# Attention block's drain: batches 3 to 5 placed before the last residual, second choices placed in a step of their own

## The chip, the cores and the metric

The kernel runs on one core of a Trainium2 chip. The metric is the device time of one execution in microseconds; the number given for a kernel is the median of its runs. A core has five engines that run side by side and meet only at semaphores: TensorE (PE, matrix products and transposes), VectorE (DVE), ScalarE (ACT), GpSimd (POOL, which here issues the indirect DMAs that gather and scatter rows) and SyncE (SP, which issues the plain DMAs).

## The reference

Eight batches of 512 rows with 128 columns (4096 rows in all) go through three layers, each added to its input: half an expert layer, linear attention, half an expert layer again.

```python
x = x + 0.5 * ffn(layernorm(x))          # experts
x = x + attn(layernorm(x))               # linear attention, 16 heads of 8
x = x + 0.5 * ffn(layernorm(x))          # experts again

def ffn(x):
    logits = xt @ wg                                     # [4096, 8]
    topv, topi = top_k(softmax(logits), 2)               # two experts for each row
    flat = one_hot(topi.T, 8).reshape(2 * 4096, 8)       # all first choices, then all second ones
    pos = sum((cumsum(flat, axis=0) - 1) * flat)         # place of the row in its expert's buffer
    valid = pos < 1024                                   # capacity; what is over is dropped
    disp[topi, pos] = xt ; y = relu(disp @ w1 + b1) @ w2 + b2
    return sum(gate * y[topi, pos])
```

What matters here is the order in the running sum: the place of a first choice depends on the first choices of the rows before it only; the place of a second choice depends on all first choices and on the second ones before it.

## The kernel before

The program has four blocks one after the other: the first routing, the first expert layer, attention with the second routing, and the second expert layer. `f` in the code is 0 for the first expert layer and 1 for the second. A batch g is four tiles of 128 rows, tiles 4g to 4g+3; all of x stays on chip in `x_sb`.

The attention block is a software pipeline over the batches, written out by hand as one list for each engine; an engine does its list strictly in order. For a batch: DVE adds the gathered expert rows to x (`add_rows`), gives statistics; ACT normalises; PE transposes and projects to q, k, v (`q`, `kv`), makes the key sums (`keysum`) and the answers (`query`); DVE divides (`divide`, L1425); PE turns and projects the result (`turn_out`, `project`, L1205 and L1209); DVE adds it to x (`residual`, L1431) and takes row statistics (`statistics`, L1437). After the loop over the batches comes the drain: what is left of batches 6 and 7, and of the routing.

The second routing runs in the same block behind it (class `Route`). For each batch PE turns x (`turn`, L467) and makes logits (`row_logits`, L479), ACT copies both (`turned_out` L426, `raw_out` L431). Then, for a part of the batches (`PARTS[1]`: part 0 is batches 0 to 2, part 1 batches 3 to 5, part 2 batches 6 and 7), DVE makes

- the mean and inverse deviation of each row from the statistics (`row_scalar_steps`, L253 to L295, small dependent steps on 8 or 12 columns),
- the two choices (`top2_steps`, L557 to L590; L575 gives the first choice and the semaphore `first_chosen`),
- the places (`place_steps`, L692 to L722) out of counts that PE makes with a triangular matrix and one of ones (`early_counts` L667 and L668, `late_counts` L674 and L675); L702 is the scan that reads them, L722 gives `place` and the semaphore `rows_placed`,
- the gap of the two logits (`gap_steps`, L728 and L733), of which ACT takes the exponential (`scalar_gate`, L451), and then gate and target number of each row, written beside the row (`first_marks`, L741 to L750).

These are Python generators: the list of DVE weaves the steps of two or three of them together, since each waits for its own step before. ACT writes the normalised rows (`scalar_norm`, L416).

POOL runs `dispatch`. For a part it waits for `rows_placed`, for both marks and, batch by batch, for the rows (`norm_act`); then it issues one indirect DMA for each tile, which scatters 128 rows to `xs_dram` at their places (L770, 32 for the first choices). Then the marks are rewritten for the second choice (`second_marks`, L759 and L760, which wait until the first scatters of that part have landed), and 32 more scatters go out (L775).

The second expert layer starts with a read of `xs_dram` (SP, `sync_rows`, L839), which waits for all 64 scatters. Before it PE does 36 transposes that serve nothing but to keep it busy (`WARM`, L948); they wait for the 28th scatter of a second choice. Then come sixteen steps of 512 rows (L904 to L940), the scatter of the results (L880) and the sums (L863).

Before the change part 2 places the first choices of batches 6 and 7 and all second choices in one step (40 columns of tiles), since `last_part` in `place_steps` stands for part 2.

Of the kernel before, what the change touches and what calls it, by code (L numbers as in the profile page):

```python
# [30 lines left out]
P = 128  # L31
NB, SEQ, C = 8, 512, 128
N = NB * SEQ
NT = N // P
GT = SEQ // P
NG = NT // GT
E, K, H = 8, 2, 512
# [4 lines left out]
PARTS = ((0, NG // 2, NG), (0, NG - 5, NG - 2, NG))  # L42
# [36 lines left out]
def finish(steps):  # L79

    for _ in steps:
        pass


def advance(steps, n):

    for _ in range(n):
        next(steps, None)


def macaron(nc, x_in, Wq, bq, Wk, bk, Wv, bv, Wo, bo, wg, w1, b1, w2, b2, out):
    ctx = ExitStack()
    with ctx:
        def sb(name, shape, dt=F32):
            return ctx.enter_context(nc.sbuf_tensor(name, shape, dt))
# [35 lines left out]
        token_id = sb("token_id", [P, NT])  # L131
        token_row = sb("token_row", [P, K, NT])
        carry = sb("carry", [P, E, K * NT])
        carry_early = [sb(f"carry_early{p}", [P, E, GT * PARTS[1][p + 1]]) for p in range(2)]
        head_mask = sb("head_mask", [P, HEADS])
        block_mask = sb("block_mask", [P, P])
        zeros = sb("zeros", [P, GT, C])
# [220 lines left out]
        class Route:  # L358
# [302 lines left out]
            def early_counts(self, pe, part):  # L661

                n = GT * PARTS[1][part + 1]
                pe.wait_ge(first_chosen, part + 1)
                pe.wait_ge(qT_ready, NG - 1 + part)
                by_expert = self.choice[:, 0:n].rearrange("p j e -> p e j")
                nc.tensor.matmul(bank[1][:, 0:E * n].rearrange("p (e j) -> p e j", e=E), tri[:], by_expert, start=True, stop=True)  # L667
                nc.tensor.matmul(bank[1][:, 256:256 + E * n].rearrange("p (e j) -> p e j", e=E), ones_bf[:], by_expert, start=True, stop=True).then_inc(counts_done, 1)  # L668
# [8 lines left out]
            def place_steps(self, dve, ch, part):  # L677
# [1 line left out]

                last_part = part == len(PARTS[1]) - 2
                n = K * NT if last_part else GT * PARTS[1][part + 1]
                js = slice(GT * PARTS[1][part], n)
                w = js.stop - js.start
# [76 lines left out]
            def dispatch(self, gp):  # L762

                for part in range(3):
                    gp.wait_ge(rows_placed, part + 1)
                    gp.wait_ge(first_marked, 2 * part + 2)
                    for g in range(PARTS[1][part], PARTS[1][part + 1]):
                        gp.wait_ge(norm_act, NG + g + 1)
                        for t in range(GT * g, GT * g + GT):
                            gp.indirect_dma_start(out=xs_dram, out_offset=bass.IndirectOffsetOnAxis(ap=self.place[:, t:t + 1], axis=0),  # L770
                                                  in_=self.xns[:, g, t % GT], in_offset=None).then_inc(firsts_in[part], 16)
                for part in range(3):
                    gp.wait_ge(second_marked, 2 * part + 2)
                    for t in range(GT * PARTS[1][part], GT * PARTS[1][part + 1]):
                        gp.indirect_dma_start(out=xs_dram, out_offset=bass.IndirectOffsetOnAxis(ap=self.place[:, NT + t:NT + t + 1], axis=0),  # L775
                                              in_=self.xns[:, t // GT, t % GT], in_offset=None).then_inc(seconds_in[t // (NT - GT)], 16)
# [344 lines left out]
        class Attention:  # L1121
# [21 lines left out]
            def tensor(self, pe):  # L1143
# [56 lines left out]
                def project(n):  # L1200
                    if n >= 1:
                        pe.wait_ge(x_summed, n)
                    if n >= 2:
                        pe.wait_ge(raw_ready, min(n - 1, NG - 3))
                    nc.tensor.matmul(bank[7].rearrange("p (t c) -> p t c", c=C), ones2[:], bpair[:].unsqueeze(1).to_broadcast([2, GT, C]), start=True, stop=False)  # L1205
                    pe.wait_ge(attT_ready, n + 1)
                    for t in range(GT):
                        at = slice(t * P, (t + 1) * P)
                        last = nc.tensor.matmul(bank[7][:, at], self.attT[:, n % 2, at], WT[:, 3], start=False, stop=(t == GT - 1))  # L1209
                    last.then_inc(o_ready, 1)  # L1210
# [30 lines left out]
                project(NG - 2)  # L1241
                turn_out(NG - 1)
                project(NG - 1)
                self.route.turn(pe, NG - 2)
                self.route.row_logits(pe, NG - 2)
                self.route.turn(pe, NG - 1)
                self.route.row_logits(pe, NG - 1)
                self.route.early_counts(pe, 1)
                self.route.late_counts(pe)

            def scalar(self, act):
# [37 lines left out]
                def attT_out(n):  # L1289
                    act.wait_ge(att_turned, n + 1)  # L1290
                    if n >= 2:
                        act.wait_ge(o_ready, n - 1)
                    nc.scalar.copy(self.attT[:, n % 2], bank[6][:]).then_inc(attT_ready, 1)
# [26 lines left out]

                self.route.raw_out(act, NG - 3)
                attT_out(NG - 1)
                self.route.turned_out(act, NG - 2)
                self.route.raw_out(act, NG - 2)
                self.route.turned_out(act, NG - 1)
                self.route.raw_out(act, NG - 1)
                self.route.scalar_norm(act, 3)
                self.route.scalar_norm(act, 4)
                self.route.scalar_gate(act, 1)
                self.route.scalar_norm(act, 5)  # L1330
                self.route.scalar_gate(act, 2)
                self.route.scalar_norm(act, 6)
# [2 lines left out]
            def vector(self, dve, ch):  # L1335
# [146 lines left out]
                den_max(NG - 2)  # L1482
                den_inverse(NG - 2)
                divide(NG - 2)
                k_sum(NG - 1)
                q_sum(NG - 1)
                kv_mask(NG - 1)
                advance(scalars, 8)
                den_max(NG - 1)
                den_inverse(NG - 1)  # L1490
                divide(NG - 1)
                residual(NG - 2)
                statistics(NG - 2)
                advance(scalars, 3)
                residual(NG - 1)
                statistics(NG - 1)
                ranks = route.top2_steps(dve, ch, 1)
                for _ in scalars:
                    advance(ranks, 1)
                scalars = row_scalar_steps(ch, dve, GT * PARTS[1][2], NT)  # L1500
                for _ in ranks:
                    advance(scalars, 2)
                finish(route.gap_steps(dve, ch, 1))
                placing = route.place_steps(dve, ch, 1)
                for _ in placing:
                    advance(scalars, 1)
                finish(scalars)
                ranks = route.top2_steps(dve, ch, 2)
                for _ in route.first_marks(dve, ch, 1):
                    advance(ranks, 1)  # L1510
                finish(ranks)
                placing = route.place_steps(dve, ch, 2)
                for _ in route.gap_steps(dve, ch, 2):
                    advance(placing, 1)
                advance(placing, 2)
                for _ in route.first_marks(dve, ch, 2):
                    advance(placing, 1)
                finish(placing)
                for part in range(3):
                    route.second_marks(dve, part)  # L1520

# [200 lines left out]
```

## Time and profile before

| | |
|---|---|
| median of 3 runs | 512.05 us (510.95 to 512.68) |
| the profiled execution | 511.76 us |
| its span in the trace | 509.9 us, 1.86 us less than its time |
| PE busy | 331.7 us, 65% |
| DVE busy | 339.5 us, 67% |
| ACT busy | 236.2 us, 46% |
| POOL busy | 270.9 us, 53% |
| 64 scatters of rows (L770, L775) | 62.1 us of POOL |
| 64 scatters of results (L880) | 70.3 us of POOL |

The span is what the trace covers; the device time is a little more. No engine is busy for the whole span, so the busy shares don't say what sets the end. In the map of the span in 40 slices (12.75 us each) PE is at nought tenths in slices 25 to 28, about 306 to 357 us: there only POOL works. The scatters of the second routing lie at 279 to 369 us. What a change there is worth is read from that stretch alone.

### The profile page before, as it was taken

The numbers are of one execution on the slowest core, as the hardware profiler recorded it, in microseconds if no ns is written. First come the engines' busy times: TensorE is split into PE (matmuls) and PEld (weight loads), VectorE is DVE, ScalarE is ACT, GpSimd is POOL, SyncE is SP. The second block draws the span as 40 slices with busy tenths as digits, with TensorE's granted clock in tenths as the row PEclk, the third lists the DMA queues.
The fourth block names the chain that finished last, engine by engine and source line by source line (L and its number), as shares of the span: only waits on it lengthen the run. The fifth ranks groups of instructions, "written<-read, shape, count | busy, mean of one in ns | idle before, by whom it ended". The sixth has DMA issues, their size and how long they took to land. (4 is left out here: it accounts for less than half of the span.)

```text
span 509.9 us, 5878 instructions
## 1 busy us (share of the span) xinstructions
PE 331.7 (65%) x1679; PEld 266.7 (52%) x1679; DVE 339.5 (67%) x1035; ACT 236.2 (46%) x430; POOL 270.9 (53%) x302
## 2 busy tenths in 40 slices
PE   7913489999999205678779830000479999999600
PEld 6902178888888103556657710000458888888400
DVE  6788579888787325689989782000057888888673
ACT  3687056666666103456548451000046666666200
POOL 9000777655630077667650737777603666666730
PEclk9999999999999755799988955555589999999955
DMA  8920114665554412112110101111131222221399
GB/s 238 356 90 0 37 50 145 194 187 183 188 189 158 163 51 53 47 46 53 42 42 1 54 22 52 52 54 52 51 127 36 84 81 82 84 63 41 117 335 282
DMA packets 43632, 53.32 MB, mean 105 GB/s; under 512 B 6646, under 2 KB 27152, under 8 KB 43600
## 3 DMA queue, kind: packets, MB, share of 16 engines
q1 hardware_dynamic: 30720, 33.69, 20.2%
q0 software_dynamic: 8512, 17.15, 11.6%
q10 hardware_dynamic: 4368, 2.10, 1.4%
q8 instruction: 14, 0.23, 0.2%
q14 instruction: 18, 0.15, 0.1%
HBM read 25.52 MB, written 27.39 MB: 104 GB/s over the span
## 5 line engine op out<-in xcount | busy, mean ns | idle before, releaser
L981 ACT ACTIVATE hf<-psum,bcol 128x512 f32<-128x512 f32 x128 | 88.5, 692 | 65.5 <-PE psum L918 62.4
L890 POOL DMA_INDIRECT xg<-xn_dram,gidx x64 | 65.1, 1017 | 68.1 <-POOLq L1541 38.0
L880 POOL DMA_INDIRECT yt_dram<-y_sb,target x64 | 70.3, 1099 | 51.8 <-DVE y_sb L1031 36.5
L1018 DVE TENSOR_TENSOR hl<-hf,hh 128x512 fp32r<-128x512 f32 x128 | 87.0, 692 | 4.5 <-ACT hh L983 2.0
L1118 POOL DMA_INDIRECT yg<-y_dram,slot x64 | 60.7, 949 | 25.1 <-issue 18.7
L916 PE MATMUL psum<-xh,wres 128*128 128x512 f32 x128 | 54.9, 429 | 2.8 <-DVE xl L1007 2.8
L1007 DVE TENSOR_TENSOR xl<-psum,xh 128x512 fp32r<-128x512 f32 x32 | 21.9, 684 | 51.9 <-ACT xh L966 51.9
L966 ACT CAST xh<-psum 128x512 fp32r<-128x512 f32 x32 | 18.8, 588 | 75.9 <-PE psum L904 73.7
L929 PE MATMUL psum<-hh,wres 128*128 128x512 f32 x128 | 52.8, 413 | 0.0
L918 PE MATMUL psum<-xh,wres 128*128 128x512 f32 x128 | 51.6, 403 | 0.0
L917 PE MATMUL psum<-xl,wres 128*128 128x512 f32 x128 | 51.6, 403 | 0.0
L930 PE MATMUL psum<-hl,wres 128*128 128x512 f32 x128 | 50.3, 393 | 0.0
L931 PE MATMUL psum<-hh,wres 128*128 128x512 f32 x128 | 50.3, 393 | 0.0
L1011 DVE CAST hh<-hf 128x512 fp32r<-128x512 f32 x96 | 41.7, 435 | 12.0 <-ACT hf L981 10.1
L770 POOL DMA_INDIRECT xs_dram<-xns,place x32 | 31.1, 971 | 32.5 <-DVE xns L750 15.8
L948 PE MATMUL psum<-ident 128*128 128x128 f32 x36 | 5.6, 333 | 58.7 <-DMA xs_dram<-xns,place 58.7
L948 PEld LDWEIGHTS psum<-ident 128*128 128x128 f32 x36 | 5.4, 178 | 60.5 <-DMA xs_dram<-xns,place 60.5
L775 POOL DMA_INDIRECT xs_dram<-xns,place x32 | 31.0, 969 | 9.8 <-issue 9.4
L1343 DVE SCALAR_TENSOR_TENSOR x_sb<-yg,gate,x_sb 128x128 f32<-128x128 f32 x64 | 18.1, 344 | 21.5 <-DMA yg<-y_dram,slot 21.4
L1257 ACT ACTIVATE an<-x_sb,rsa 128x128 f32<-128x128 f32 x32 | 13.2, 484 | 36.4 <-DVE rsa L1387 36.4
L916 PEld LDWEIGHTS psum<-xh,wres 128*128 128x128 f32 x128 | 25.1, 196 | 7.9 <-DVE xl L1007 3.4
L918 PEld LDWEIGHTS psum<-xh,wres 128*128 128x128 f32 x128 | 24.9, 194 | 6.1
(221 smaller groups left out, 734.6 us busy)
## 6 DMA issues: line engine op xcount, KB each, us to landing
yt_dram<-zeros SPq DMA_DIRECT2D x24, 256.0 KB, 3.4
ring<-yt_dram SPq DMA_DIRECT2D x24, 256.0 KB, 5.0
xs_dram<-blank SPq DMA_DIRECT2D x16, 260.0 KB, 3.1
xg<-xs_dram SPq DMA_DIRECT2D x16, 260.0 KB, 2.7
wexp_raw<-in_L_ffn_w SPq DMA_DIRECT2D x16, 256.0 KB, 6.0
y_dram<-y_sb SPq DMA_DIRECT2D x16, 256.0 KB, 2.4
x_sb<-in_L_attn_x SPq DMA_DIRECT2D x8, 256.0 KB, 4.0
xn_dram<-xns SPq DMA_DIRECT2D x8, 256.0 KB, 6.2
```

The lines of the kernel that those rows point to most:

```text
L880: gp.indirect_dma_start(out=yt_dram, out_offset=bass.IndirectOffsetOnAxis(ap=target[:, j:j + 1], axis=0), in_=self.y_sb[:, s % YG, t], in_ ...
L890: gp.indirect_dma_start(out=self.xg[:, s % 4, t], out_offset=None, in_=xn_dram, in_offset=bass.IndirectOffsetOnAxis(ap=gidx[:, j:j + 1], a ...
L916: nc.tensor.matmul(bank[1 + c][:], w[:, 0, at], self.xh[:, s % 2], start=True, stop=False)
L917: nc.tensor.matmul(bank[1 + c][:], w[:, 0, at], self.xl[:, s % 2], start=False, stop=False)
L918: nc.tensor.matmul(bank[1 + c][:], w[:, 2, at], self.xh[:, s % 2], start=False, stop=True).then_inc(h_ready[c], 1)
L929: nc.tensor.matmul(sums[:], w[:, 1, at], self.hh[:, s % 2, c], start=(c == 0), stop=False)
L930: nc.tensor.matmul(sums[:], w[:, 1, at], self.hl[:, s % 2, c], start=False, stop=False)
L931: last = nc.tensor.matmul(sums[:], w[:, 3, at], self.hh[:, s % 2, c], start=False, stop=(c == HC - 1))
L981: one = nc.scalar.activation(self.hf[:, c], bank[1 + c][:], ACT.Relu, bias=bcol[:, at:at + 1])
L1011: dve.tensor_copy(self.hh[:, s % 2, c], self.hf[:, c]).then_inc(hh_ready[c], 1)
L1018: dve.tensor_tensor(self.hl[:, s % 2, c], self.hf[:, c], self.hh[:, s % 2, c].bitcast(F32), ALU.subtract).then_inc(hl_ready[c], 1)
L1118: gp.indirect_dma_start(out=self.yg[:, n % YB, k, t], out_offset=None, in_=y_dram, in_offset=bass.IndirectOffsetOnAxis(ap=slot[:, k, GT * ...
```

## The change

Five things are changed:

- The second choices become a fourth step of placing: `last_part` is now part 3 with 32 columns, and part 2 places the 8 tiles of batches 6 and 7 alone, with a third mask `carry_early` (128 partitions x 256 elements, set once at the start of the kernel).
- PE makes counts for part 1 right after the projection of batch 7, before batch 6 is turned for the routing, and a third pair of early counts for part 2.
- ACT normalises batches 3 and 4 and takes the exponential for part 1 before it copies the turned rows of batches 6 and 7.
- DVE starts on the row scalars of part 1 sooner, chooses and places part 1 between the division of batch 7 and the last residual, and does part 2 and the second choices after that.
- POOL waits for the fourth `rows_placed` before the first scatter of a second choice.

```diff
-                pe.wait_ge(qT_ready, NG - 1 + part)
+                pe.wait_ge(qT_ready, NG - 1 if part == 0 else NG)
+                if part > 0:
+                    pe.wait_ge(counts_read, part)
...
-                last_part = part == len(PARTS[1]) - 2
+                last_part = part == len(PARTS[1]) - 1
...
+                gp.wait_ge(rows_placed, 4)
                 for part in range(3):
                     gp.wait_ge(second_marked, 2 * part + 2)
...
                 project(NG - 1)
+                self.route.early_counts(pe, 1)
                 self.route.turn(pe, NG - 2)
...
-                self.route.early_counts(pe, 1)
+                self.route.early_counts(pe, 2)
                 self.route.late_counts(pe)
...
                 attT_out(NG - 1)
+                self.route.scalar_norm(act, 3)
+                self.route.scalar_gate(act, 1)
+                self.route.scalar_norm(act, 4)
                 self.route.turned_out(act, NG - 2)
...
                 divide(NG - 2)
+                advance(scalars, 6)
                 k_sum(NG - 1)
                 q_sum(NG - 1)
                 kv_mask(NG - 1)
-                advance(scalars, 8)
+                advance(scalars, 6)
                 den_max(NG - 1)
                 den_inverse(NG - 1)
                 divide(NG - 1)
+                ranks = route.top2_steps(dve, ch, 1)
+                advance(ranks, 3)
                 residual(NG - 2)
-                statistics(NG - 2)
-                advance(scalars, 3)
-                residual(NG - 1)
-                statistics(NG - 1)
...
+                placing = route.place_steps(dve, ch, 1)
+                for _ in route.gap_steps(dve, ch, 1):
+                    advance(placing, 1)
+                advance(placing, 3)
+                for _ in route.first_marks(dve, ch, 1):
+                    advance(placing, 1)
+                finish(placing)
+                residual(NG - 1)
+                statistics(NG - 2)
+                statistics(NG - 1)
...
+                finish(route.place_steps(dve, ch, 3))
                 for part in range(3):
                     route.second_marks(dve, part)
```

On DVE before the change, from the division of batch 7 (L1425) on: both residuals (L1431) with their statistics come first, then the choices of part 1 (L557 to L575).

```order
L1425 TENSOR_TENSOR att<-psum,den 128x512
L1431 TENSOR_TENSOR x_sb<-psum,x_sb 128x512
L1437 BN_STATS stats<-x_sb 128x6 x4
L291 SCALAR_TENSOR_TENSOR nw<-nw 128x12
...
L1431 TENSOR_TENSOR x_sb<-psum,x_sb 128x512
L1437 BN_STATS stats<-x_sb 128x6 x4
L291 SCALAR_TENSOR_TENSOR nw<-nw 128x12
L557 TENSOR_REDUCE first<-raw 128x12
```

After the change, the same engine from the same division on (L1429 and L1435 are the same lines, four further down; `first` and `top` are maxima of the choosing, `place` the result of placing part 1):

```order
L1429 TENSOR_TENSOR att<-psum,den 128x512
L557 TENSOR_REDUCE first<-raw 128x12
L561 TENSOR_TENSOR ranked<-raw,first 128x96
L565 TENSOR_TENSOR ranked<-ranked,prefer 128x96
L1435 TENSOR_TENSOR x_sb<-psum,x_sb 128x512
L569 TENSOR_REDUCE top<-ranked 128x12
...
L752 TENSOR_SCALAR xns<-gap 128x12
L724 TENSOR_TENSOR place<-valid,slotf 128x12
L1435 TENSOR_TENSOR x_sb<-psum,x_sb 128x512
L1441 BN_STATS stats<-x_sb 128x6 x8
```

One residual and eight statistics now stand behind the placing of part 1 instead of ahead of its first step; the other residual stands inside the choosing.

On PE before, from the projection of batch 7 on (L1209): two batches turned and their logits, then the counts of part 1 (192 columns) and the late counts (512).

```order
L1209 MATMUL psum<-WT,attT 128x128 x4
L467 MATMUL psum<-ident,x_sb 128x128 x4
L479 MATMUL psum<-wgc,xT 128x8 x4
L467 MATMUL psum<-ident,x_sb 128x128 x4
L479 MATMUL psum<-wgc,xT 128x8 x4
L667 MATMUL psum<-choice,tri 128x192
L668 MATMUL psum<-choice,ones_bf 128x192
L674 MATMUL psum<-choice,tri 128x512
L675 MATMUL psum<-choice,ones_bf 128x512
```

After, from the same projection on (L1212); L669 and L670 are the early counts:

```order
L1212 MATMUL psum<-WT,attT 128x128 x4
L669 MATMUL psum<-choice,tri 128x192
L670 MATMUL psum<-choice,ones_bf 128x192
L467 MATMUL psum<-ident,x_sb 128x128 x4
L479 MATMUL psum<-wgc,xT 128x8 x4
L467 MATMUL psum<-ident,x_sb 128x128 x4
L479 MATMUL psum<-wgc,xT 128x8 x4
L669 MATMUL psum<-choice,tri 128x256
L670 MATMUL psum<-choice,ones_bf 128x256
L676 MATMUL psum<-choice,tri 128x512
L677 MATMUL psum<-choice,ones_bf 128x512
```

The counts of part 1 moved ahead of four groups of matrix products, and a pair with 256 columns is new.

## Rows read from the trace of the kernel before

**Rows 1.** Chain that ended last, 366 to 373 us: start, us, what.

```profile
366.84 2.34 DMA xs_dram<-xns,place
369.28 2.74 DMA xg<-xs_dram
372.06 0.67 PE psum L904 x4
```

**Rows 2.** Timeline of POOL: start, us, instruction, [idle before it <- releaser].

```profile
279.31 1.01 POOL L770 DMA_INDIRECT xs_dram<-xns,place  x1 [15.82 <-DVE xns L750]
...
293.38 0.97 POOL L770 DMA_INDIRECT xs_dram<-xns,place  x1 [0.30 <-issue]
301.88 0.97 POOL L770 DMA_INDIRECT xs_dram<-xns,place  x1 [7.53 <-ACT xns L416]
...
326.09 0.97 POOL L770 DMA_INDIRECT xs_dram<-xns,place  x1 [0.30 <-issue]
...
366.84 0.97 POOL L775 DMA_INDIRECT xs_dram<-xns,place  x1 [0.30 <-issue]
```

**Rows 3.** Timeline of DVE, 278 to 301 us.

```profile
278.32 0.18 DVE L750 TENSOR_SCALAR xns<-gap 128x12 f32<-128x12 f32 x1
...
285.41 0.17 DVE L253 TENSOR_TENSOR nw<-stats 128x12 f32<-128x12 f32 x1
...
287.53 0.22 DVE L1414 TENSOR_SCALAR den<-psum 128x64 f32<-128x64 f32 x1
...
288.37 0.69 DVE L1425 TENSOR_TENSOR att<-psum,den 128x512 f32<-128x512 f32 x1
289.13 0.69 DVE L1431 TENSOR_TENSOR x_sb<-psum,x_sb 128x512 f32<-128x512 f32 x1
...
291.64 0.69 DVE L1431 TENSOR_TENSOR x_sb<-psum,x_sb 128x512 f32<-128x512 f32 x1 [0.41 <-PE psum L1209]
...
293.23 0.25 DVE L557 TENSOR_REDUCE first<-raw 128x12 f32<-128x96 f32 x1
...
293.51 0.26 DVE L561 TENSOR_TENSOR ranked<-raw,first 128x96 f32<-128x96 f32 x1
...
297.82 0.25 DVE L693 TENSOR_TENSOR pos<-choice,expert_base 128x96 f32<-128x96 bf16 x1
...
298.46 0.56 DVE L702 TENSOR_TENSOR_SCAN cum<-psum,carry_early 128x191 f32<-128x191 f32 x1
...
300.33 0.17 DVE L722 TENSOR_TENSOR place<-valid,slotf 128x12 int32<-128x12 f32 x1
...
300.96 0.17 DVE L750 TENSOR_SCALAR xns<-gap 128x12 f32<-128x12 f32 x1
```

**Rows 4.** Timeline of PE, 285 to 297 us.

```profile
285.54 1.25 PE L1189 MATMUL psum<-kv,qT 128*128 128x144 f32 x8 [0.46 <-DVE kv L1410]
...
287.93 1.16 PE L1209 MATMUL psum<-WT,attT 128*128 128x128 f32 x8
...
290.45 1.16 PE L1209 MATMUL psum<-WT,attT 128*128 128x128 f32 x8
291.44 0.60 PE L467 MATMUL psum<-ident,x_sb 128*128 128x128 f32 x4
...
296.17 0.50 PE L667 MATMUL psum<-choice,tri 128*128 128x192 bf16 x1
296.49 0.52 PE L668 MATMUL psum<-choice,ones_bf 128*128 128x192 bf16 x1
```

**Rows 5.** Timeline of ACT, normalised rows of batches 3 and 4.

```profile
296.44 3.19 ACT L416 ACTIVATE xns<-x_sb,nmr,rstd 128x128 f32<-128x128 f32 x8
```

**Rows 6.** Stretches: length, busy PE, PEld, DVE, ACT, POOL, clock, DMA, GB/s.

```profile
196.00:213.50 17.50, 12.13 (x36) 8.49 (x37) 10.38 (x49) 5.77 (x11) 12.60 (x14) 0.60 0.19 51
374.00:377.40 3.40, 3.28 (x10) 2.69 (x11) 0.98 (x4) 1.27 (x2) 0.00 (x0) 0.50 0.34 129
```

**Rows 7.** Timeline of POOL in the expert layer, 470 us.

```profile
470.58 1.36 POOL L880 DMA_INDIRECT yt_dram<-y_sb,target  x1 [0.30 <-issue]
```

More of the change, by code:

```diff
@@ L133, in macaron @@
         carry = sb("carry", [P, E, K * NT])
-        carry_early = [sb(f"carry_early{p}", [P, E, GT * PARTS[1][p + 1]]) for p in range(2)]
+        carry_early = [sb(f"carry_early{p}", [P, E, GT * PARTS[1][p + 1]]) for p in range(3)]
         head_mask = sb("head_mask", [P, HEADS])
@@ L1326, in scalar @@
                 self.route.raw_out(act, NG - 1)
-                self.route.scalar_norm(act, 3)
-                self.route.scalar_norm(act, 4)
-                self.route.scalar_gate(act, 1)
                 self.route.scalar_norm(act, 5)
@@ L1491, in vector @@
                 divide(NG - 1)
+                ranks = route.top2_steps(dve, ch, 1)
+                advance(ranks, 3)
                 residual(NG - 2)
-                statistics(NG - 2)
-                advance(scalars, 3)
-                residual(NG - 1)
-                statistics(NG - 1)
[L1497 to L1500, printed above, removed]
                 for _ in ranks:
[L1502 to L1505, printed above, removed]
                     advance(scalars, 1)
                 finish(scalars)
+                placing = route.place_steps(dve, ch, 1)
[8 more added lines that the diff above has]
+                statistics(NG - 1)
+                scalars = row_scalar_steps(ch, dve, GT * PARTS[1][2], NT)
                 ranks = route.top2_steps(dve, ch, 2)
-                for _ in route.first_marks(dve, ch, 1):
-                    advance(ranks, 1)
-                finish(ranks)
+                advance(scalars, 4)
+                for _ in ranks:
+                    advance(scalars, 1)
+                finish(scalars)
                 placing = route.place_steps(dve, ch, 2)
@@ L1514, in vector @@
                     advance(placing, 1)
-                advance(placing, 2)
+                advance(placing, 3)
                 for _ in route.first_marks(dve, ch, 2):
```

## The prediction

> **What bounds the kernel now.** I read the chain of waits first, then the timeline of POOL through the second routing, and then what DVE, PE and ACT do while POOL stands still. The chain ends the attention block with POOL's last scatter of rows, its landing, one read by SP and the first transposes of the expert layer [rows 1]. Nothing else stands in that chain for a long way back: the issues of the 64 scatters follow each other. From the issue at 326.09 to the last one at 366.84 there are 32 steps [rows 2], so one costs 40.75/32 = 1.273 us. Only two breaks are in the row of 64: the start, and 7.53 us ahead of 301.88. Part 0 (12 scatters, 279.31 to 293.38) is done by 294.35, and part 1 is not ready. From 301.88 on POOL never stops: 51 steps of 1.274 us make 64.96, which is 366.84. So each microsecond by which the issue at 301.88 comes sooner moves the last one by a microsecond, as long as every later part is ready in time. At most 7.53 - 0.30 = 7.23 us can be had, since 0.30 us lies between any two issues.
>
> What does POOL wait for at 301.88? The row names ACT's normalised rows. But the first four scatters of part 1 need batch 3 only, and batches 3 and 4 were written from 296.44 to 299.63 [rows 5], so ACT had long been done for them. What came last is DVE: place at 300.33 + 0.17 = 300.50 and the marks at 300.96 + 0.17 = 301.13 [rows 3]. From the marks to the issue is 0.75 us; for part 0 it is 279.31 - 278.50 = 0.81 [rows 2, 3]. I take 0.78 from "ready" to "issued".
>
> **Where DVE loses its time before, and when part 1 is ready after.** All times are those of the profiled execution.
>
> Step 1, the division. PE's answers for batch 7 end at 285.54 + 1.25 = 286.79 [rows 4], but DVE reads them at 287.53 [rows 3], because eight steps of row scalars stand ahead, from 285.41 on, 2.12 us. Six steps now go before the keys of batch 7, into idle time of DVE, and only six are left here; the dependent ones take 0.2 us each, 1.2 in all. DVE reads at about 286.85, 0.68 us sooner; the division, at 288.37 before, starts at 287.69. Its next instruction can start 0.64 us later, 288.33.
>
> Step 2, three steps of choosing. One dependent step on 96 elements takes 293.51 - 293.23 = 0.28 us [rows 3], with small steps woven in or not; I take 0.29. The third starts at 288.9, and the residual of batch 6 at 289.15. PE's projection for it ends at 287.93 + 1.16 = 289.09 [rows 4], so it isn't waited for, and the residual is where it was (289.13). It holds DVE 0.6 us, to 289.75. Thus PE's projection of batch 7, which needs that residual, stays at 290.45 to 291.61.
>
> Step 3, the rest of the choosing: seven steps of 0.29 and 0.16 to the next free instruction make 2.19, to 291.94; the first instruction of placing starts at 292.03. Before it was at 297.82. The 5.8 us between are the two statistics and the last residual, which waited 0.41 us for PE [rows 3], the row scalars of part 2, and the 0.68 of step 1: all of that now stands behind.
>
> Step 4, placing and marks: before it is 2.68 us from 297.82 to the end of place and 3.31 to the end of the marks, which came last. Now marks and placing are woven, so place ends last: 292.03 + 2.65 = 294.68. With 0.78 the issue comes at 295.46 instead of 301.88: **6.42 us sooner**. POOL would still be idle for 1.1 us.
>
> What must be there by then: (a) The scan L702 comes 0.6 us after placing starts, 292.6; PE's counts follow the projection of batch 7, can start at 291.44 like the transposes there before, and took 0.84 us from 296.17 to 297.01 [rows 4]: 292.3, a margin of 0.3 us, the smallest. It delays the turning of batch 6 by as much, which isn't on the path. (b) ACT's rows of batch 3: the row scalars end at 291, four activations take half of 3.19 us [rows 5], 292.6, then the exponential 0.2; DVE asks for it at 293.8. Margin 1 us. (c) Part 2 must be ready 12 issues after 295.46, that is by 310.7 - 0.8 = 309.9. DVE: last residual and eight statistics to 297.1. ACT copies the turned rows of batch 6 only at 294.4 (behind batch 4) and the residual of batch 7 comes 3 us later than before; turning and logits of 7 then take 2.9 us, so raw logits at 298.9. Ten steps of choosing 3.0, placing of 8 tiles about 2.8: 304.7. Margin 5 us, so the longer way costs nothing. (d) The second choices need 32 columns placed after that, below 5.6 us, 310.3, and are asked for at 295.46 + 20 x 1.273 - 0.8 = 320.1. The new wait on POOL thus costs nothing; nothing but those 32 scatters is queued behind it. (e) New work: a third mask at the start of the kernel and a pair of matmuls, beside work that isn't waited for; between 0 and 0.5 us, the longer of the marks of the mask being POOL's alone; I take 0.
>
> What POOL gives back then passes on: the last landing, SP's read and PE's start depend on nothing that stays in place, and the expert layer behind is one rigid piece. Span 509.9 - 6.42 = 503.5, and with the 1.86 outside the trace 505.3. The profiled execution (511.76) is 0.29 under the median of the runs (512.05), so for the median **505.6 us**.
>
> **A rule to weigh.** In these rows each of the twelve scatters of part 0 took 0.97 to 1.01 us while DVE was at work nearly all the time, and in the expert layer one took 1.36 [rows 2, 7]. The Trainium skill (SBUF — State Buffer, Who interferes with whom) says that a copy, cast or tensor_scalar of VectorE can hold the port through which GpSimd writes descriptors, and then the issue waits. By that rule POOL's issues at 295 to 310 us, which move beside a DVE that is placing, would be longer. The small steps of the routing didn't do that before, so the trace speaks against it here; the fourth rival below prices it.
>
> **Rivals.**
> 1. More is gained. If the reckoned 294.68 is a microsecond too late, POOL's pause closes: 7.23 us, 504.8. Beside it the clock: at the start of the expert layer PE ran at the lower level, 1.2 GHz (0.50), for the 3.4 us from 374.0 with PE busy for 3.28 [rows 6]. Had it not fallen after the 36 transposes, half of that, 1.7 us, is won too: 503.1. The transposes move with the scatters, so I see no reason for either sign, and hold it as spread.
> 2. Less is gained. The margin (a) of 0.3 us fails, or the chain on DVE is longer than its steps, or the clock rises 3.3 us later in the expert layer (1.65 us lost). For it: four engines hand over to each other within 8 us. One to three us: 506.8 to 508.6.
> 3. Nothing or a loss: the clock. The restart of PE in the attention block had a mean of 0.60 over 17.5 us with PE busy for 12.1 [rows 6]. If the expert layer, now begun at another moment, stood at 1.2 GHz for long, every microsecond there would cost half a one. The point is 13 us beyond the 3.4: then the 6.42 are gone; at 20 us the time is 505.6 + 10 = 515.6. Against it: PE was busy without a break from 374.12 on, and rose at 377.4.
> 4. The port. 11 issues between 295.5 and 309.9, each longer by 1.36 - 0.97 = 0.39, cost 4.3 us: 509.9.
> 5. The change does not do what it says, because part 2 is late. It would have to come at 309.9 + 6.4 = 316.3 to take all, 11.6 us after what I reckon.
>
> **How the numbers follow.** Forecast 505.6 with its own range 504.4 to 506.8 (0.6 for the steps, as much for the clock and the spread of the runs): 0.70. Rival 1: 0.12. Rival 2: 0.11. Rival 4: 0.02. Rivals 3 and 5: 0.05, of which 0.03 end slower and 0.02 within 0.3%. A measurement of this kernel can tell 0.3% (1.5 us) from no change. For 8 in 10 the range reaches into rivals 1 and 2: 503.7 to 508.2. Faster by over 0.3% (under 510.5) are the forecast, 1, 2 and 4: 0.95; same 0.02; slower 0.03.
>
> **What would show it.** POOL's thirteenth scatter of rows starts near 295.5 with an idle of 1.1 us before it, and 51 steps of 1.27 us follow without a break to about 360.4. On DVE the first line of choosing starts near 288.3, placing near 292.0, place ends near 294.7. PE's counts of part 1 end by 292.3. The first transposes of the expert layer are at 365.6 instead of 372.06. Step 1 is wrong if the division doesn't move; step 3 if DVE waits for raw logits or for the residual's projection; (a) if the scan has idle time with PE as its releaser; (c) or (d) if POOL pauses a second time. The whole is wrong if the expert layer takes longer than before from its first transposes on.

## The result

| | before | changed |
|---|---|---|
| median | 512.37 us (510.95 to 512.88, 4 runs) | 505.59 us (505.11 to 509.36, 4 runs) |
| profiled execution | 511.76 us, span 509.9 us | 505.73 us, span 504.0 us |

The ratio is 0.989 with an interval of 0.9858 to 0.9922: faster, by 6.8 us between the medians shown. The forecast was 505.6 us. Single runs are less close to it than the median is (one of the four took 509.36 us), and so are the places in the trace, as the next section shows.

### The profile page after: what moved, and what is told of

Its sections match the earlier page's. It is cut to its first block and busy times, and to the rows that moved or that the text cites. A ratio compares the mean times of both kernels' runs of the same rounds, so it can differ in the third digit from the quotient of the medians.

```text
span 504.0 us, 5897 instructions
## 1 busy us (share of the span) xinstructions
PE 335.8 (67%) x1681; PEld 272.3 (54%) x1681; DVE 340.9 (68%) x1045; ACT 236.0 (47%) x430; POOL 272.4 (54%) x304
## 5 line engine op out<-in xcount | busy, mean ns | idle before, releaser
L919 PE MATMUL psum<-xh,wres 128*128 128x512 f32 x128 | 54.6, 426 | 2.8 <-DVE xl L1010 2.8
L1154 PE MATMUL psum<-ident,an 128*128 128x128 f32 x32 | 7.8, 391 | 31.8 <-ACT an L1261 26.6
L919 PEld LDWEIGHTS psum<-xh,wres 128*128 128x128 f32 x128 | 24.8, 193 | 7.8 <-DVE xl L1010 3.4
```

The costliest lines, as they stand in the source:

```text
L919: nc.tensor.matmul(bank[1 + c][:], w[:, 0, at], self.xh[:, s % 2], start=True, stop=False)
```

## The profile after the change

The chain that ended last, at the end of the attention block. Columns: start us, us, what. It answers to [rows 1]:

```profile
361.39 2.29 DMA xs_dram<-xns,place
363.70 0.03 SPq L837
363.77 2.59 DMA xg<-xs_dram
366.40 0.67 PE psum L907 x4
```

The last scatter comes 5.45 us sooner (361.39 against 366.84) and the first transposes of the expert layer 5.66 us sooner (366.40 against 372.06). From there to the end of the span it is 137.6 us, and 137.8 before. So nothing was given back in the expert layer.

The timeline of POOL around its pause (start, us, instruction, idle before it and releaser), for [rows 2]:

```profile
278.58 1.01 POOL L772 DMA_INDIRECT xs_dram<-xns,place  x1 [15.69 <-DVE xns L752]
...
292.67 0.97 POOL L772 DMA_INDIRECT xs_dram<-xns,place  x1 [0.30 <-issue]
296.31 0.97 POOL L772 DMA_INDIRECT xs_dram<-xns,place  x1 [2.67 <-DVE place L724]
297.59 0.97 POOL L772 DMA_INDIRECT xs_dram<-xns,place  x1 [0.30 <-issue]
```

One pause, 2.67 us instead of 7.53, then 51 steps of 1.276 us to 361.39 without a second one. The releaser named is now DVE's place, and place is indeed what ended last.

What DVE did (for [rows 3]; L1400 makes the keys of batch 7, L1429 divides, L1435 is the residual, L695 starts placing):

```profile
284.10 0.69 DVE L1400 SCALAR_TENSOR_TENSOR kk<-psum,ke 128x512 f32<-128x512 f32 x1 [0.47 <-ACT vv L1291]
...
288.60 0.69 DVE L1429 TENSOR_TENSOR att<-psum,den 128x512 f32<-128x512 f32 x1
289.20 0.24 DVE L557 TENSOR_REDUCE first<-raw 128x12 f32<-128x96 f32 x1
...
290.05 0.69 DVE L1435 TENSOR_TENSOR x_sb<-psum,x_sb 128x512 f32<-128x512 f32 x1
...
292.97 0.25 DVE L695 TENSOR_TENSOR pos<-choice,expert_base 128x96 f32<-128x96 bf16 x1
...
293.61 0.56 DVE L704 TENSOR_TENSOR_SCAN cum<-psum,carry_early 128x191 f32<-128x191 f32 x1
...
295.51 0.17 DVE L724 TENSOR_TENSOR place<-valid,slotf 128x12 int32<-128x12 f32 x1
295.60 0.68 DVE L1435 TENSOR_TENSOR x_sb<-psum,x_sb 128x512 f32<-128x512 f32 x1
...
305.65 0.17 DVE L724 TENSOR_TENSOR place<-valid,slotf 128x8 int32<-128x8 f32 x1
```

From the division to place no instruction of DVE, shown here or left out, has an idle time in brackets: DVE's own chain fills these 7.1 us. The last residual stands directly behind place. Part 2 is placed at 305.82.

PE and ACT in the same stretch (for [rows 4] and [rows 5]; L669 and L670 are the counts of part 1, L416 writes normalised rows):

```profile
291.22 1.16 PE L1212 MATMUL psum<-WT,attT 128*128 128x128 f32 x8
292.21 0.50 PE L669 MATMUL psum<-choice,tri 128*128 128x192 bf16 x1
292.53 0.52 PE L670 MATMUL psum<-choice,ones_bf 128*128 128x192 bf16 x1
```

```profile
291.89 1.65 ACT L416 ACTIVATE xns<-x_sb,nmr,rstd 128x128 f32<-128x128 f32 x4 [0.82 <-DVE nmr L295]
...
299.94 0.19 ACT L431 COPY raw<-psum 128x32 f32<-128x32 f32 x1 [1.97 <-PE psum L479]
300.02 1.65 ACT L416 ACTIVATE xns<-x_sb,nmr,rstd 128x128 f32<-128x128 f32 x4
```

The counts end at 293.05 and the scan starts at 293.61. ACT writes the rows of batch 3 by 293.5, those of batch 5 by 301.7.

Last, the clock. The stretches of 4 us in which PE works for batch 7, first of the kernel before, then of the changed one (length, busy PE, PEld, DVE, ACT, POOL, granted clock, DMA share, GB/s):

```profile
276.00:280.00 4.00, 4.00 (x30) 3.58 (x30) 3.77 (x19) 2.70 (x8) 0.69 (x1) 1.00 0.00 0
```

```profile
276.00:280.00 4.00, 4.00 (x19) 3.76 (x20) 3.23 (x16) 1.58 (x5) 1.12 (x2) 0.57 0.00 0
```

PE is busy for all 4 us in both, at 1.00 in one and mostly at the lower level (1.2 GHz) in the other, with 19 instead of 30 matmuls. In the 2 us before it, from 274 to 276, PE was busy for 1.44 and 1.46 us and the clock was 1.00 in both. Nothing that was changed in the lists stands before that stretch. What it costs can be read from POOL's first scatter to the keys of batch 7. That is 3.86 to 3.88 us in the five traces in which the clock from 276 to 280 us was 1.00 (the kernel before, and of the experiments below the fourth step alone, the last residual first, placing before the division, 60 transposes). It is 5.47 to 5.52 us in the five in which it was 0.57 to 0.72 (the changed kernel, the order alone, the counts late, both residuals, the copies). So the lower clock goes with 1.6 us. The changed kernel had begun this stretch 0.73 us sooner in its trace (278.58 against 279.31), and its keys came 0.92 us later (284.10 against 283.18). Why the clock fell in some executions and not in others isn't shown.

## The experiments

All are compared with the kernel before, run beside them on the same chip. Its median was 512.02 us beside the first four, 511.91 beside the next four, 554.57 beside the three that can't be read and 511.86 beside the last.

### The fourth step of placing alone

```diff
 # the order of before on DVE, ACT and PE, and in it:
-                last_part = part == len(PARTS[1]) - 2
+                last_part = part == len(PARTS[1]) - 1
...
+                self.route.early_counts(pe, 2)
                 self.route.late_counts(pe)
...
                 finish(placing)
+                finish(route.place_steps(dve, ch, 3))
...
+                gp.wait_ge(rows_placed, 4)
```

> The order of before on every engine, and only the second choices placed in a fourth step of their own. Theory (the gain is the earlier first scatter of part 1 alone): no change, 512.4 us within 0.3%, and POOL's pause before its thirteenth scatter stays at 7.5 us, since part 2 was ready about 8 us early already. Rival (the smaller placing of part 2 is worth something by itself): 1 to 2 us faster, 510.5 to 511.5.

Measured: 512.41 us (511.78 to 514.33), ratio 1.001 (0.9994 to 1.0025). POOL's pause in its timeline:

```profile
302.23 0.97 POOL L772 DMA_INDIRECT xs_dram<-xns,place  x1 [7.54 <-ACT xns L416]
```

The same pause, and no change: this part of the diff is worth nothing by itself.

### The order alone

```diff
 # the changed kernel, and in it:
-                last_part = part == len(PARTS[1]) - 1
+                last_part = part == len(PARTS[1]) - 2
...
-                gp.wait_ge(rows_placed, 4)
...
-                self.route.early_counts(pe, 2)
                 self.route.late_counts(pe)
...
-                finish(route.place_steps(dve, ch, 3))
```

> The new order on DVE, ACT and PE, but part 2 places 40 columns in one step as before, without the fourth step. Theory: the whole gain, 505.6 us (505 to 506.6); part 2 is ready about 2 us later than in the changed kernel (near 308 us), still 3 us before POOL asks for it, and POOL stands still once only. Rival (the fourth step is needed so that POOL doesn't stop a second time): a second pause before the 25th scatter, 507 to 508 us.

Measured: 505.72 us (504.36 to 507.63), ratio 0.9877 (0.9853 to 0.99). Two lines of its trace, POOL's only pause and DVE's placing of 40 columns:

```profile
295.49 0.97 POOL L772 DMA_INDIRECT xs_dram<-xns,place  x1 [2.68 <-DVE place L724]
```

```profile
307.58 0.20 DVE L724 TENSOR_TENSOR place<-valid,slotf 128x40 int32<-128x40 f32 x1
```

The whole gain is in the order. The order was changed on PE, ACT and DVE together. The next two experiments take back one piece each on PE and on DVE; what ACT's new order and the earlier row scalars are worth by themselves no run shows. The long step ends at 307.78, 2.0 us later than in the changed kernel, and POOL asks for it about 310.1 (295.49 + 12 x 1.274 = 310.8, less 0.7).

### The counts of part 1 late

```diff
                 project(NG - 1)
-                self.route.early_counts(pe, 1)
                 self.route.turn(pe, NG - 2)
                 self.route.row_logits(pe, NG - 2)
+                self.route.early_counts(pe, 1)
```

> The changed kernel, but PE makes the counts of part 1 behind the turning and the logits of batch 6. Theory (PE's counts are the input with the smallest margin, some 0.3 us): the scan of DVE waits for PE until about 297.4 instead of 293.6, all 52 scatters behind it come 3.8 us later, 509.4 us. Rival (the count's place in PE's list has slack, DVE's own chain sets the start): under 1 us lost, 505.6 to 506.6.

Measured: 508.89 us (508.14 to 510.01), ratio 0.9929 (0.9907 to 0.9951). DVE's scan now waits:

```profile
298.03 0.55 DVE L704 TENSOR_TENSOR_SCAN cum<-psum,carry_early 128x191 f32<-128x191 f32 x1 [3.99 <-PE psum L670]
```

The loss against 505.59 is 3.3 us for 3.99 us of wait. The rival falls. PE's counts must not stand behind the turning of batch 6.

### The last residual first

```diff
                 residual(NG - 2)
+                residual(NG - 1)
+                statistics(NG - 2)
+                statistics(NG - 1)
                 for _ in ranks:
                     advance(scalars, 1)
...
                 finish(placing)
-                residual(NG - 1)
-                statistics(NG - 2)
-                statistics(NG - 1)
```

> The changed kernel, but the last residual and the eight statistics stand between the third and the fourth step of choosing part 1, so ahead of its placing. Theory (step 3 of the prediction): the residual waits for PE's projection until 292.4, statistics end at 294.7, so place comes 4.0 us later and the time is 509.6 us; batches 6 and 7 are ready sooner, which is worth nothing. Rival (the gain came from the earlier start of row scalars and choosing, not from the place of the last residual): within 1 us of the changed kernel, 505.6 to 506.6.

Measured: 508.36 us (507.27 to 509.13), ratio 0.9922 (0.9899 to 0.9946). DVE's division, the residual and place:

```profile
287.66 0.69 DVE L1429 TENSOR_TENSOR att<-psum,den 128x512 f32<-128x512 f32 x1
...
291.48 0.69 DVE L1435 TENSOR_TENSOR x_sb<-psum,x_sb 128x512 f32<-128x512 f32 x1 [1.68 <-PE psum L1212]
...
298.45 0.17 DVE L724 TENSOR_TENSOR place<-valid,slotf 128x12 int32<-128x12 f32 x1
```

From the division to the end of place it is 10.96 us instead of 7.08: 3.88 more, as expected (4.0). The medians differ by 2.8 us only. The traces say where the difference is: in this one the division itself came 0.94 us sooner than in the trace of the changed kernel, with PE's clock at 1.00 from 276 to 280 us instead of 0.57. So place ended 2.94 us later, POOL's thirteenth scatter came 2.95 us later (299.26), and the span is 2.5 us longer. That the medians differ for the same reason isn't shown.

### Both residuals behind the placing

```diff
                 advance(ranks, 3)
-                residual(NG - 2)
...
                 finish(placing)
-                residual(NG - 1)
+                residual(NG - 2)
                 statistics(NG - 2)
+                residual(NG - 1)
...
-                project(NG - 1)
                 self.route.early_counts(pe, 1)
+                project(NG - 1)
```

> The changed kernel, but the residual of batch 6 too stands behind the placing of part 1, and PE makes the counts of part 1 ahead of the projection of batch 7. Theory (what still stands in DVE's chain before place costs its own length): place 0.6 us sooner, POOL's pause 2.1 instead of 2.7 us, 505.0 us. Rival (something else, as ACT's rows or the exponential, sets the start by now): no change, 505.6 us.

Measured: 506.62 us (504.52 to 508.63), ratio 0.9891 (0.9855 to 0.9927). The first pause is as expected, but there is a second one, before the first scatter of batch 5:

```profile
295.54 0.97 POOL L772 DMA_INDIRECT xs_dram<-xns,place  x1 [2.07 <-DVE place L724]
...
307.30 0.97 POOL L772 DMA_INDIRECT xs_dram<-xns,place  x1 [1.86 <-ACT xns L416]
```

And this is why, on PE and ACT:

```profile
295.56 0.79 PE L1208 MATMUL psum<-bpair,ones 2*128 2x512 f32 x1 [4.23 <-DVE x_sb L1435]
...
303.38 1.88 PE L479 MATMUL psum<-wgc,xT 128*128 128x8 f32 x8 [0.68 <-ACT xT L426]
```

```profile
305.30 0.19 ACT L431 COPY raw<-psum 128x32 f32<-128x32 f32 x1 [1.97 <-PE psum L479]
305.38 1.65 ACT L416 ACTIVATE xns<-x_sb,nmr,rstd 128x128 f32<-128x128 f32 x4
```

The rows of batch 5 stand behind the raw logits of batch 7 in ACT's list. The residual that moved came at 294.82 instead of 290.05, 4.77 us later, and held up PE's projection of batch 7 for 4.23 us. ACT had the raw logits of batch 7 5.36 us later than in the changed kernel (305.30 against 299.94). The clock adds little to that: it was 0.50 from 295 to 300 us here, so the logits of batch 6 took 1.88 us instead of 1.06, but those of batch 7 took 1.88 us in the changed kernel too. What was won in front (0.6 us) is lost behind. Neither theory nor rival had that.

### Placing before the division

```diff
                 keysum(NG - 1)
-                query(NG - 1)
                 self.route.row_logits(pe, NG - 3)
+                query(NG - 1)
                 project(NG - 2)
+                self.route.early_counts(pe, 1)
...
                 advance(scalars, 6)
-                den_max(NG - 1)
-                den_inverse(NG - 1)
-                divide(NG - 1)
                 ranks = route.top2_steps(dve, ch, 1)
-                advance(ranks, 3)
-                residual(NG - 2)
...
                 finish(placing)
+                den_max(NG - 1)
+                den_inverse(NG - 1)
+                divide(NG - 1)
+                residual(NG - 2)
```

The raw logits of batch 7 go to a bank of their own, ACT normalises for the gate ahead of writing the turned attention output of batch 7, and PE takes the logits of batch 6 after turning batch 7.

> A version meant to be faster: PE makes the logits of batch 5 ahead of the answers of batch 7, DVE chooses and places part 1 ahead of the division of batch 7 and of both residuals, PE turns batches 6 and 7 one after the other. Theory: place comes 2.3 us sooner than in the changed kernel, POOL's pause falls to the 0.3 us between any two issues, 503.3 us; part 2 is then ready near 306.9 us and asked for near 307.7, so the margin is small. Rival (batches 6 and 7 are now the late ones): a second pause before the 25th scatter of 1 to 3 us, 504.3 to 506.3 us.

Measured: 504.69 us (504.14 to 505.17), ratio 0.985 (0.9827 to 0.9873). No pause of POOL is left between its first scatter and its last (start 280.10 and 360.74). DVE's place and the first scatter of batch 5 (the 21st):

```profile
293.16 0.17 DVE L724 TENSOR_TENSOR place<-valid,slotf 128x12 int32<-128x12 f32 x1
```

```profile
305.87 0.97 POOL L772 DMA_INDIRECT xs_dram<-xns,place  x1 [0.30 <-issue]
```

POOL's 64 scatters take 80.64 us from first to last, and 82.81 in the changed kernel, so 2.2 us are won there, as expected. Of them 0.9 show in the medians; in this execution the first scatter itself came 1.5 us later than in the trace of the changed kernel. ACT had the rows of batch 5 written at 304.46, 0.7 us before POOL asked for them. It has the lowest median beside a kernel before of 512 us, but its interval overlaps the changed kernel's.

### Idle transposes: 60 instead of 36

```diff
-WARM = 36
+WARM = 60
```

> The changed kernel with 60 idle transposes of PE instead of 36 ahead of the second expert layer, so that PE is busy until its first rows have landed. Theory of the clock (the fall to 1.2 GHz at the layer's start costs half its length, 3.3 to 3.6 us): the granted clock stays at 1.00 from the first step on, 1.6 us faster, 504.0 us, and less spread. Rival (the transposes themselves run at 1.2 GHz and end after the rows have landed): up to 1.4 us lost, 505.6 to 507.0 us.

Measured: 506.49 us (505.84 to 508.85), ratio 0.9896 (0.987 to 0.992): not faster. The chain of its trace:

```profile
358.00 9.68 PE psum L951 x60
367.67 0.45 PE psum L907 x4
```

The theory of the clock held: over 366 to 372 us it is 1.00, and from L907 to the end of the span it is 136.4 us instead of 137.6. But the 60 transposes stand in the chain themselves: they end at 367.68, and L907 starts right behind them. One scatter landed late, too (SP's read was issued at 364.62, 3.9 us after the last issue of POOL at 360.75), but that cost nothing here. The transposes, released at 358.00 by the 28th second scatter, would have ended at 367.68 all the same.

Up to 350 us this is the changed kernel in everything, and in this trace PE's clock from 276 to 280 us was 1.00. It is a second look at the prediction's path, without the clock's fall:

```profile
287.77 0.69 DVE L1429 TENSOR_TENSOR att<-psum,den 128x512 f32<-128x512 f32 x1
...
294.67 0.17 DVE L724 TENSOR_TENSOR place<-valid,slotf 128x12 int32<-128x12 f32 x1
```

```profile
295.47 0.97 POOL L772 DMA_INDIRECT xs_dram<-xns,place  x1 [0.97 <-DVE place L724]
```

The prediction had the division at 287.69, the end of place at 294.68 (here 294.84), the thirteenth scatter at 295.46 and an idle of 1.1 us before it.

### Copies on DVE beside POOL's issues

```diff
-                for part in range(3):
+                route.second_marks(dve, 0)
+                dve.wait_ge(an_turned, NG)
+                for _ in range(30):
+                    ch.then(dve.tensor_copy(self.an[:, 0].rearrange("p t c -> p (t c)"), x_sb[:, 0:GT].rearrange("p t c -> p (t c)")))
+                for part in range(1, 3):
                     route.second_marks(dve, part)
```

> The changed kernel with 30 copies of 128x512 f32 within SBUF on DVE in the 13 us after the marks of part 0, where DVE was idle and POOL issues scatters; they compute nothing that is used. Theory (rival 4 of the prediction, the port held by copies, is real but the small steps of the routing don't hold it): the scatters beside them take longer than 0.97 us, up to 1.36 as in the expert layer, ten of them, 1 to 4 us lost, 506.6 to 509.6 us. Rival (POOL's issue doesn't depend on what DVE does): all scatters 0.97 us, 505.6 us.

Measured: 505.5 us (504.56 to 505.92), ratio 0.9864 (0.9837 to 0.9892). POOL and DVE together:

```profile
309.51 1.04 POOL L772 DMA_INDIRECT xs_dram<-xns,place  x1 [0.30 <-issue]
309.51 15.42 DVE L1530 COPY an<-x_sb 128x512 f32<-128x512 f32 x30
310.85 0.97 POOL L772 DMA_INDIRECT xs_dram<-xns,place  x1 [0.30 <-issue]
...
319.98 1.23 POOL L772 DMA_INDIRECT xs_dram<-xns,place  x1 [0.30 <-issue]
321.51 1.22 POOL L778 DMA_INDIRECT xs_dram<-xns,place  x1 [0.30 <-issue]
```

Four of the issues beside the copies take 1.22 or 1.23 us and four 1.04 instead of 0.97, together 1.3 us. Single issues of 1.03 to 1.05 us occur without copies too (placing before the division, the counts late). From POOL's thirteenth scatter to PE's first transposes it is 71.8 us (295.13 to 366.95) and 70.1 in the changed kernel. Of these 1.7 us at most 1.3 stand beside the copies; 0.4 are two longer issues (1.08 and 1.24 us) beside DVE's placing, before the copies began. The median shows no loss. The Trainium skill (SBUF — State Buffer, Who interferes with whom) says that the engine that comes second is blocked until the other's instruction is finished. The trace agrees in sign. In size, no issue was lengthened by more than 0.26 us, half the length of a copy (0.51 us); where in a copy each issue began isn't shown, so the rule's size is not tested.

### Three runs that can't be read, and one more

> The changed kernel once more, beside the two below, since the spread of its four runs (505.1 to 509.4) is as wide as the differences asked about. Theory: 505.6 us within 0.8; runs above 507 are runs in which PE's clock fell more often in the attention block or the expert layer. Rival (the first four runs were lucky): 506.5 to 508 us.

> The version that places part 1 before the division, with 48 idle transposes instead of 36, which should end near 365 us, just before the first rows of the expert layer have landed. Theory (the clock stays up if PE's idle time there is under 1 us): 503.4 to 504.2 us, 0.5 to 1.3 us faster than with 36 (504.7). Rival (the clock falls anyway, or the transposes end too late): 504.7 to 505.7 us.

> The changed kernel with 1 idle transpose instead of 36. Theory (with 36 the clock falls again while PE waits for its rows, so they bring little): the layer starts at 1.2 GHz as it does with 36, within 0.5 us, 505.6 to 506.1 us. Rival (the 36 shorten the stretch at 1.2 GHz by a third or more): 1 to 2 us slower, 506.6 to 507.6 us.

On the chip where these three ran the kernel before took 554.57 us (547.65 to 559.04), the changed kernel 548.93 (ratio 0.9896, 0.9836 to 0.9955), the version with 48 transposes 548.7 (0.986, 0.9805 to 0.9916) and the changed kernel with 1 transpose 544.94 (0.9796, 0.9721 to 0.9871). Two of the longest waits of the changed kernel in 280 to 340 us there (engine, line, releaser: us, times, longest):

```profile
POOL xs_dram L772 <- DVE place L724: 14.7, 1, 14.7
DVE kv L1413 <- remote: 9.3, 2, 8.4
```

DVE stood for 8.4 us, ahead of the division of batch 7, for something that the trace puts down to no engine of this core. Everything was 8% slower there. The ratio of the changed kernel has the sign of the first measurement, but its size isn't confirmed: five of the eleven runs of the kernel before lie more than 1.5% above its fastest, the median of the other six is 552.3 us, and against that the changed kernel is at 0.994. What the number of idle transposes is worth stays open; the kernel with 1 may even be the faster one, its interval overlaps the other two.

> The same as v4_warm48, which ran where the kernel before took 555 us: part 1 placed before the division, and 48 idle transposes. Theory: 503.4 to 504.2 us if the clock stays up at the start of the expert layer. Rival: as with 36 transposes or slower, 504.7 to 505.7 us.

Measured on a chip where the kernel before took 511.86 us: 508.06 us (506.33 to 508.99), ratio 0.9918 (0.9893 to 0.9943), 3.4 us slower than with 36 transposes. In its trace the transposes aren't the reason: they end at 367.10, and L907 starts at 368.96, when its rows have landed. POOL has two pauses again, and its last scatter landed late:

```profile
294.85 0.96 POOL L772 DMA_INDIRECT xs_dram<-xns,place  x1 [2.12 <-DVE place L724]
...
307.55 0.96 POOL L772 DMA_INDIRECT xs_dram<-xns,place  x1 [2.82 <-ACT xns L416]
```

```profile
362.29 3.88 DMA xs_dram<-xns,place
```

The lists of the two kernels differ in nothing before 350 us. In this trace the clock was 0.50 from 276 to 280 us (and POOL's first scatter to the keys of batch 7 took 7.15 us) and 0.50 from 296 to 303, in the one with 36 it was 1.00 and 0.73. The sixteen matmuls of the logits of batches 6 and 7 took 3.42 us against 1.90, and ACT had the rows of batch 5 at 307.28 against 304.46. POOL had also begun 2.4 us sooner here (277.70 against 280.10), so it asked for them sooner. The version without a pause has little slack behind batch 5 (expected: 0.8 us for part 2, and none was reckoned for ACT's rows). In this trace the slack didn't last. At the start of the expert layer the clock fell here too (0.63 from 371.0 to 375.0 us), so the theory of the 48 transposes did not hold in the profiled execution. That PE's clock is what separates the medians of 504.7 and 508 us is likely and not shown: two profiles don't settle it.

## Why the prediction was right, point by point

**What bounds the kernel.** Right, and shown both ways: the pause before the thirteenth scatter was the only thing worth shortening. Where it stayed (fourth step alone) the time stayed; where DVE's way to place was lengthened by 3.9 to 4.0 us the time rose by 2.8 and 3.3.

**Who ends the pause.** Right. ACT was named in [rows 2], and DVE's place was argued from [rows 3, 5]; the changed kernel's own row names DVE's place, with ACT's rows of batch 3 done by 293.5, nearly 3 us before.

**Step 1, the division at 287.69.** In the changed kernel's trace it is at 288.60. The step was right: DVE now waits 0.23 us for PE's answers instead of reading them late. The ground under it moved: the keys of batch 7 were 0.92 us late, by 1.65 us that go with the lower clock (5.52 against 3.87 from POOL's first scatter) less 0.73 of an earlier start. In the six other traces with the same list up to there the division is at 287.41 (copies), 287.66 (last residual first), 287.77 (60 transposes), 287.80 (order alone), 288.42 (both residuals) and 289.14 us (counts late).

**Steps 2 to 4.** Reckoned 6.99 us from the start of the division to the end of place, measured 7.08 (288.60 to 295.68). The choosing began 0.60 us after the division instead of 0.64, the placing took 2.71 instead of 2.65.

**From ready to issued.** Taken as 0.78, measured 0.63 (295.68 to 296.31). The 0.75 and 0.81 in the trace before count from the marks, which ended last there; from place it was 0.63 or 0.64 in this and seven other traces. So the issue came at 296.31 instead of 295.46, 0.85 us late: 0.91 + 0.09 - 0.15. POOL's pause was 2.67 us and not 1.1, since its first part ended 0.7 us sooner too. In the trace with 60 transposes, where the clock didn't fall from 276 to 280 us, the issue came at 295.47 after a pause of 0.97.

**What passes on.** Forecast 6.42, of which 5.57 came at that scatter, 5.45 at the last and 5.9 at the end of the span. The sum was right by 0.5 us in the span. The last scatter came 0.97 us later than forecast: 0.85 from the thirteenth, 0.12 from 51 steps that were a little longer. Then 0.45 us came back: 0.21 between that scatter and the first transposes (5.01 us instead of 5.22), and 0.24 in the expert layer. Between the medians the gain is 6.8 us; the forecast had 6.4, from a median of three runs (512.05), which is 512.37 over four. The agreement of 505.59 with 505.6 to 0.01 is chance; executions of one kernel differ by 2 us and more.

**Margins.** (a) The counts ended at 293.05 and were asked for at 293.61, margin 0.56 (reckoned 0.3); putting them late cost 3.3 us, so DVE does depend on them. (b) as reckoned: the exponential was there at 293.6, asked for at 294.8. (c) part 2 was placed at 305.82 (reckoned 304.7 with a start 0.9 us sooner) and asked for about 311, so 5 us, and 3 with 40 columns. (d) 310.0 against 321. One margin was not reckoned: the rows of batch 5, which ACT writes behind the raw logits of batch 7. It was 4 us here (301.7 against 305.8, the ninth scatter of part 1 less 0.7), and it is the one that broke in two of the later versions.

**Rivals.** The first (pause closed, clock) did not come: the pause stayed, and the clock at the start of the expert layer fell as before (0.53 from 368.5 to 372.0 us). The second is what happened in part: the thirteenth scatter came 0.85 us late, by the clock ahead of the division and not by the steps after it; for the medians it didn't come. The third did not come. The fourth is true in kind and small: at most 1.3 us for 30 copies, in the changed kernel no scatter took above 1.01 us, and in two other executions (60 transposes, and the copies) two issues beside the small placing steps took 1.08 and 1.24 us. The fifth did not come.

## What to carry to other kernels

Find the one pause in the queue that is otherwise full, and reckon the list of the engine that ends it instruction by instruction; here such a sum over 7 us held to a tenth of a microsecond, counted from its start, while the start itself moved by 0.9. When work is moved behind a critical piece, list every later consumer of every engine's list, also those that only stand behind the moved work on an engine that seems idle. A version that uses up the last slack can lose it again from one execution to the next: here it had no pause in one trace and two in another.

## What the runs showed that was not expected

- With the same lists up to there, PE ran from 276 to 280 us at 1.00 in some traces and at 0.57 to 0.72 in others, with PE busy for 3.7 to 4 of the 4 us. From POOL's first scatter to the keys of batch 7 it was 3.9 us in the first and 5.5 in the second.
- The clock at the start of the expert layer didn't always fall. In five traces the 36 transposes ended 2.0 to 2.3 us before L907 (the kernel before, the changed one, the fourth step alone, the order alone, placing before the division), and the clock was 0.57 or 0.58 over 4 us from the layer's first L919 (L916 before) on. In four they ran longer, 6.3 to 7.1 us instead of 5.6 to 5.8, ended 0.7 to 1.5 us before L907, and it was 1.00 (counts late, last residual first, both residuals, copies).
- The median scatter landed in 2.3 or 2.4 us, but some took up to 4.7 (4.2 in the changed kernel's trace). Since the next stage waits for all 64, one late landing near the end can count whole: 1.6 us with 48 transposes (3.88 against 2.29). With 60 transposes it hid behind them.
- POOL's issue began 0.63 or 0.64 us after place when place came last (eight traces), and 0.75 to 0.81 us after the marks when they did.
- Beside copies within SBUF on DVE, four indirect issues on POOL took 1.04 us and four 1.22 or 1.23 instead of 0.97.
